# A routed feed-forward and biased attention kernel: trees routed by products, denser slots for tree groups and attention tiles

## What is computed

```python
# attention: x is (4, 512, 128), 16 heads of 8
xn = layernorm(x)                                  # both parts start from normalised tokens
scores = q @ k.T * scale + relative_position_bias  # per batch and head, 512 x 512
out = softmax(scores) @ v @ w_proj.T + b_proj
# feed-forward: four binary trees q, k, v, f of depth 8, over 2048 tokens
for _ in range(8):
    logit = (x * nw[node]).sum(-1) + nb[node]
    node = 2 * node + 1 + (logit > 0)
leaf = node - 255                                  # 256 leaves
y_tree = relu(x @ w1[leaf] + b1[leaf]) @ w2[leaf] + b2[leaf]     # gelu in tree f
# attention over the FFN's tokens: softmax(q k.T / sqrt(128)) v, added to xn, gives y; then y + tree_f(y)
# the output is the sum of both parts
```

## Time and profile before

| | |
|---|---|
| median of 3 runs | 713.75 us (712.23 to 715.29) |
| the profiled execution | 716.28 us, its span 714.6 us |
| PE busy | 576.0 us (81%) |
| DVE busy | 441.7 us (62%) |
| ACT busy | 336.8 us (47%) |
| POOL busy | 255.1 us (36%) |
| mean granted PE clock | 0.942 of 2.4 GHz |

### The profile page before, as it was taken

How to read it: one execution, slowest core, us unless ns; L and a number is a source line. 1 busy time by engine, 2 the same in 40 slices (tenths; PEclk the granted TensorE clock), 3 DMA queues, 4 the chain that set the end, 5 groups by cost and what they waited for, 6 DMA issues and landing times.

```text
span 714.6 us, 11516 instructions
## 1 busy us (share of the span) xinstructions
PE 576.0 (81%) x3540; PEld 413.1 (58%) x3540; DVE 441.7 (62%) x1024; ACT 336.8 (47%) x738; POOL 255.1 (36%) x242
## 2 busy tenths in 40 slices
PE   2276644799999999999999898998976898989930
PEld 0164532577777777776767655656643466666620
DVE  2959987657576666666667556555768565555300
ACT  5520001455555545464646554545223378878720
POOL 4401766750006578267003820000000776000285
PEclk9998758899999999999999999999999799999985
DMA  7979541275657778788551210000000357445123
GB/s 222 253 170 218 215 134 44 54 198 154 163 148 207 195 196 164 184 186 188 155 160 42 34 16 15 1 1 1 0 1 0 112 111 168 133 134 143 41 34 76
DMA packets 108828, 83.42 MB, mean 117 GB/s; under 512 B 8688, under 2 KB 105840, under 8 KB 108768
## 3 DMA queue, kind: packets, MB, share of 16 engines
q1 hardware_dynamic: 93472, 70.07, 37.0%
q0 software_dynamic: 15104, 12.63, 9.6%
q10 hardware_dynamic: 192, 0.00, 0.0%
HBM read 58.30 MB, written 24.36 MB: 116 GB/s over the span
## 4 chain that ended last, share of the span: by engine, by line
PE 59%; DVE 8%; issue 5%; ACT 5%; POOL 4%; DMA 0%; POOLq 0%; DVEq 0%; ACTq 0%
PE ps L983 8%; PE ps L960 7%; PE ps L971 7%; PE ps L973 7%; PE ps L1037 7%; PE ps L1047 6%; POOL xr L386 3%; PE ps L943 3%; DVE ps L618 2%; PE ps L1090 2%; PE ps L1042 2%; ACT hr L797 2%; PE ps L1031 2%; PE ps L998 1%; PE ps L1097 1%
## 5 line engine op out<-in xcount | busy, mean ns | idle before, releaser
L618 DVE CUSTOM_DVE_ANT_0 ps<-ps,strip 128x512 f32<-128x512 f32 x256 | 176.9, 701 | 132.7 <-PE ps L960 128.4
L786 ACT ACTIVATE pt<-ps 128x512 f32<-128x512 f32 x256 | 150.7, 600 | 91.1 <-PE ps L973 89.4
L381 POOL DMA_INDIRECT xs<-xr,slot x64 | 63.4, 990 | 244.6 <-issue 154.8
L971 PE MATMUL ps<-qs,km 128*128 128x512 f32 x256 | 127.1, 497 | 8.4 <-ACT pt L786 7.5
L960 PE MATMUL ps<-km,qs 128*128 128x512 f32 x256 | 111.8, 443 | 15.9 <-DVE mx L618 7.4
L386 POOL DMA_INDIRECT yt<-ys,slot x48 | 74.6, 1555 | 80.5 <-DMA ys<-yl 66.5
L797 ACT ACTIVATE hr<-ps,wt 128x128 f32<-128x128 f32 x192 | 54.7, 368 | 68.0 <-PE ps L1037 68.0
L973 PE MATMUL ps<-u_lo,rev_r 128*128 128x220 f32 (+1 forms) x256 | 74.5, 291 | 0.0
L973 PE MATMUL ps<-u_hi,rev_r 128*128 128x220 f32 (+1 forms) x256 | 73.2, 286 | 0.0
L983 PE MATMUL ps<-pt,v_aug 128*32 128x512 f32 x512 | 69.0, 612 | 0.7 <-ACT pt L786 0.7
L971 PEld LDWEIGHTS ps<-qs,km 128*128 128x128 f32 x256 | 49.0, 191 | 31.2 <-ACT pt L786 19.6
(11 more groups left out here) (207 smaller groups left out, 864.2 us busy)
## 6 DMA issues: line engine op xcount, KB each, us to landing
wt<-in_wl SPq DMA_DIRECT2D x192, 128.5 KB, 2.4
xl<-xs SPq DMA_DIRECT2D x48, 258.0 KB
ys<-yl SPq DMA_DIRECT2D x48, 256.0 KB
xs<-mx SPq DMA_DIRECT2D x2, 3096.0 KB, 23.7
strip<-bias_bf SPq DMA_DIRECT2D x1, 3584.0 KB, 36.2
u_hi<-bias_hi SPq DMA_DIRECT2D x1, 2496.0 KB, 16.1
u_lo<-bias_lo SPq DMA_DIRECT2D x1, 2496.0 KB, 28.5
xs<-xr,slot POOLq DMA_INDIRECT x64
```

Of the source, the lines that this page charges most:

```text
L381: pool.indirect_dma_start(out=xs[t % 2][:, :], out_offset=bass.IndirectOffsetOnAxis(ap=slot[:, t, k:k + 1], axis=0), in_=xr[:, k, :], in_o ...
L618: V.tensor_tensor_reduce(out=bank(u % banks), in0=bank(u % banks), in1=strip[:, HG * g + j, b0:b0 + NS], scale=1.0, scalar=LOWEST, op0=ALU ...
L786: A.activation(pt[:, kt % 2, j, :], bank(2 + u % 2), ACT.Exp).then_inc(S["ex"], 1)
L971: T.matmul(bank(2 + u % 2), km[:, par, j, kt * P:(kt + 1) * P], qs[:, par, :], start=True, stop=False)
```

## The change

It has four parts.

1. **Routing by products.** The logits come out transposed (nodes on partitions, tokens on the free axis). DVE compares two tiles of 128x512 per chunk of 512 tokens (`bits_of`). PE multiplies the bits with a constant path table (`follow`); ACT turns the sums into a one-hot of leaves with a Relu (`leafT`); PE multiplies that with a block table (`settled`), which gives block and leaf. The three trees run as one pipeline of 12 chunks. POOL builds the tables (`tree_edges`, `tree_rows`) and copies the leaf column into the rows ahead of a scatter; before, DVE did, behind a wait for the last scatter.
2. **Tree groups every three slots**, h one slot behind x instead of two, and y four behind instead of five; the groups start 16 slots ahead of slot 0, during the first step's `scores_q`, which go back to two banks.
3. **FFN attention** takes a tile every two slots instead of 2.5, with "o" three slots behind "s"; each batch of values has its own semaphore (`g_v0` to `g_v3`). The eight transposes go one a slot.
4. As a consequence tree f is routed from slot 138 instead of 209 and its groups start at slot 190 instead of 252; the last slot with FFN work is 227 of 320, before 301.

```diff
-LOGIT_BANKS = (2, 3, 4, 5, 6, 7, 0, 1)
+LOGIT_BANKS = ((2, 3), (4, 5))
+PATH_BANKS = (6, 7)
-STAGE_AT = {"x": 0, "h": 2, "m": 3, "y": 5}
-EVERY = 4
-QK_FROM, ATT_FROM, ROUTE_FROM, F_FROM = 150, 167, 209, 252
-ATT_PE, ATT_DVE, ATT_ACT = {"s": 0, "p": 2, "o": 4}, {"s": 0, "o": 4}, {"s": 1, "p": 2}
+STAGE_AT = {"x": 0, "h": 1, "m": 2, "y": 4}
+EVERY = 3
+TREES_FROM, QK_FROM, ATT_FROM, ROUTE_FROM, F_FROM = -16, 95, 103, 138, 190
+ATT_PE, ATT_DVE, ATT_ACT = {"s": 0, "p": 2, "o": 3}, {"s": 0, "o": 3}, {"s": 1, "p": 2}
...
-        for first, start, count in ((0, 0, NTREE * GROUPS), (NTREE * GROUPS, F_FROM, GROUPS)):
+        for first, start, count in ((0, TREES_FROM, NTREE * GROUPS), (NTREE * GROUPS, F_FROM, GROUPS)):
...
-    t, rest = divmod(slot_ - QK_FROM, 2)
-    return [t] if rest == 0 and 0 <= t < 2 * NB else []
+    t = slot_ - QK_FROM
+    return [t] if 0 <= t < 2 * NB else []
...
-    return [(k, i) for i in range(NT) for k, d in reversed(delays.items()) if ATT_FROM + 5 * i // 2 + d == slot_]
+    return [(k, i) for i in range(NT) for k, d in reversed(delays.items()) if ATT_FROM + 2 * i + d == slot_]
...
+            def tree_edges():
+
+                settle(G.iota(n1, [[P, 2]], base=1, channel_multiplier=1, allow_small_or_imprecise_dtypes=True))
+                settle(G.iota(row, [[1, LEAVES]], base=0, channel_multiplier=0, allow_small_or_imprecise_dtypes=True))
+                settle(G.memset(wd, float(LEAVES)))
+                for lv in range(1, 8):
+                    settle(G.tensor_scalar(one, n1, float(1 << lv), -float(1 << (8 - lv)), ALU.is_ge, ALU.mult))
+                    settle(G.tensor_tensor(wd, wd, one, ALU.add))
...
+            def tree_rows():
+
+                b8 = row.rearrange("p (j r) -> p j r", r=LB)[:, :, 0]
+                for h in range(2):
+                    settle(G.tensor_scalar(paths[:, h], row, mid[:, h:h + 1], 2.0, ALU.is_ge, ALU.mult))
+                    for edge in (first, end):
+                        settle(G.tensor_scalar(tmp, row, edge[:, h:h + 1], None, ALU.is_ge))
+                        settle(G.tensor_tensor(paths[:, h], paths[:, h], tmp, ALU.subtract))
...
+                pool.sem_inc(S["tc"], 1)
...
+                settle(G.tensor_copy(xr[:, :, P], part_of[:, t, :]))
...
+            tree_edges()
             far_rows()
+            tree_rows()
...
-                V.tensor_copy(slot[:, t, :], st[:, 5, :])
-                if t:
-                    dve.wait_ge(S["d_sc"], 16 * NT * t)
-                V.tensor_copy(xr[:, :, P], whole[:, 0:NT]).then_inc(S["sl"], 1)
+                V.tensor_copy(slot[:, t, :], st[:, 5, :]).then_inc(S["sl"], 1)
...
+            def bits_of(i):
+
+                t, c = divmod(i, CHUNKS)
+                for h in range(2):
+                    dve.wait_ge(S["lg"], 2 * i + h + 1)
+                    V.tensor_scalar(bitsT[:, h, c * NS:(c + 1) * NS], bank(LOGIT_BANKS[i % 2][h]), nbT[:, t, h:h + 1], None,
+                                    ALU.is_gt).then_inc(S["bit"], 1)
...
+            for i in range(NTREE * CHUNKS + 3):
+                if i < NTREE * CHUNKS:
+                    bits_of(i)
+                t, c = divmod(i, CHUNKS)
+                if c == 1 and t > 0:
+                    places(t - 1, t1)
+                if c == 2 and t > 0:
+                    for _ in ranked(t - 1, t1, (0, 1)):
+                        pass
...
+            def logits(i):
+
+                t, c = divmod(i, CHUNKS)
+                if i >= 2:
+                    pe.wait_ge(S["bit"], 2 * i - 2)
+                for h in range(2):
+                    T.matmul(bank(LOGIT_BANKS[i % 2][h]), nws[t][:, h * P:(h + 1) * P], xn2T[:, c * NS:(c + 1) * NS],
+                             start=True, stop=True).then_inc(S["lg"], 1)
...
+            def settled(i):
+
+                t, c = divmod(i, CHUNKS)
+                pe.wait_ge(S["oh"], 2 * i + 2)
+                if c == 0 and t > 0:
+                    pe.wait_ge(S["rt"], t)
...
+            pe.wait_ge(S["tc"], 1)
...
+            for i in range(NTREE * CHUNKS + 3):
+                if i < NTREE * CHUNKS:
+                    logits(i)
+                t, c = divmod(i, CHUNKS)
+                if c == 2 and t > 0:
+                    ranks(t - 1, t1, (0, 1))
+                if 1 <= i <= NTREE * CHUNKS:
+                    follow(i - 1)
+                if 2 <= i <= NTREE * CHUNKS + 1:
+                    settled(i - 2)
...
-            for u in range(U):
-                scores_q(0, u, 0, 4)
+            for at in range(SLOTS):
+                if at >= LAG:
+                    scores_q(0, at - LAG, 0)
+                for k, i in stages(slot_of(-1, at)):
+                    stage(k, i, i % 2)
```

167 lines of the change are left out of this document (110 added, 57 removed).

## The result

The change makes the kernel slower. The changed kernel took 731.5 us in the median of 4 runs (729.3 to 741.0) against 713.7 for the kernel before in the same session, a ratio of 1.024 with an interval of 1.020 to 1.027. A second session gave 734.5 us and 1.027 (1.024 to 1.031). The prediction was 703 with a range of 684 to 719. The profile shown is that of the second session (the run a0_after_again, the same kernel, span 731.9 us), because the profiled execution of the first session was a slow one (741.0 us, left out of the ratio).

A forecast was written before the change was run, and what follows sets the result against it. PE was taken as the limit in the three trees' stretch, chains and POOL's last gathers elsewhere. Terms -12 + 18 + 44.5 - 42 - 19 = -10.5 gave 705.8 from 716.28, or 703 from the 713.75 median; range 684 to 719.

The forecast's parts named there:

- routing: Ahead of the main loop: routing by products brings the first `scores_q` at 107.5 instead of 119.5, -12 us, bounds -5 and -17.
- the slots ahead of step 0: Slots -16 to -1: three group loops at 6.8 us, 20.4 in all; +18 us for this stage, step 0 at 141.
- slots 0 to 93: Stretch of the three trees' groups: 203 us long against 158.5, +44.5 us, of which 22 are waiting.
- behind slot 94: Rest of the main loop, before 390.7 us: no tree groups -31, attention tiles -11, tree f's groups -1, transposes +1; -42.
- the end: After the main loop: `add_out` no longer waits for POOL's gathers and starts 0.1 us after its product, -19.0 us.
- I take 6.4 us a group: Tree groups: y of one group, weight loads, then h two groups later form a loop of 6.2 to 6.6 us.
- Rival 2: Tree groups: weight-loading loop gets longer, POOL's gathers beside it; a loss from 6.7 us a group, worst 732; chance 0.13.
- a slot without FFN work costs 1.085 us, 21.7 a step: Main loop: slots 0 to 93 less 23.25 groups at 2.43 us of PE leave 102 us for 94 slots.
- I expect 1.9: FFN attention tiles: from 2.6 to 1.9 us each with "o" ahead of the next "p", -11 us, between -15 and +3.
- Tree f's groups: Behind slot 94: 12 groups took 41 us; ACT is the limit, so a group's cost stays, -2 to +6, taken as -1.
- Routing of tree f: Behind slot 94: 29 us before, the same DVE chain after, so no change.
- The 2.4 us for a lower clock at the start of routing: Start of routing: PE comes from idle, so the first 5 us run at the lower clock level, costing 2.4 us.

The follow-up runs named there:

- h1: Changed kernel with three of four of GpSimd's gathers for the trees left out, scatters kept (FFN output not the reference's): 724.1 us, ratio 1.012.
- g2: e1 with only the three trees' groups every third slot, y of a group issued ahead of h of the next: 696.7 us, ratio 0.975.
- f4: Changed kernel with FFN attention as before, a tile every two and a half slots, tree f's routing and groups eight slots later: 735.5 us, ratio 1.029.
- f1: Changed kernel with all schedule numbers of the kernel before; routing by products, leaf column on GpSimd and finer gather semaphores stay: 702.8 us, ratio 0.984.
- e1: Changed kernel with tree groups every four slots, the stage delays of before, and later starts for attention and tree f: 674.0 us, ratio 0.944.
- g1: e1 with its first group in slot 0 instead of -16 and all that follows 16 slots later: 689.8 us, ratio 0.966.
- e2: Changed kernel with y of a group issued ahead of h of the next group in the same slot: 697.8 us, ratio 0.975.
- f2: e2 with weights loaded only for the first two groups of the trees and of tree f (FFN output not the reference's): 675.5 us, ratio 0.947.
- f3: Changed kernel without token-row loads behind the first two groups of the trees and of tree f (FFN output not the reference's): 729.8 us, ratio 1.024.
- h2: e2 with three of four of GpSimd's gathers for the trees left out (FFN output not the reference's): 688.3 us, ratio 0.963.

## Why the prediction was wrong

The sum is made against the profiled executions: 705.8 us less 1.7 around the span is 704.1, and the span is 731.9, 27.8 above. By the prediction's own terms: routing +2.6 better, the slots ahead of step 0 2.3 worse, slots 0 to 93 14.0 worse, behind slot 94 17.2 worse, the end 3.0 better.

**The failed step is the loop, "I take 6.4 us a group".** The mechanism was right: each of its members stands in the fences above. Its size was that of an undisturbed loop. By the rows, from y to the first issue 1.24, the issues 1.93, then 2.2 or 2.8 to h, and 1.0 from h to y: 6.4 without GpSimd's transfers beside it and 7.0 with them. The prediction had 6.2 with the median landing and 6.6 with 2.9 for the latest of four, took the middle, and did not ask what GpSimd's queue does in the same stretch, though 17 of the 24 loops that waited had its transfers beside the gap. The measured mean is 6.95, and y(35) comes at 358.3, where 143.5 + 198 + 2 = 343.5 was foretold.

The 31 distances from y(4) to y(35) sum to 215.5 us, for 200.4. One is 10.9, at the batch's border, where 8.4 was allowed; one is 8.9; the last is only 3.7, since no h stands in front of y(35). The 28 others are 6.86 in the mean and make 12.8 of the 15.1 us. Slots 0 to 93 took 217.0 us for 203. Of these 14 us, h1 gives 6.2 back (349.2 less 138.4 is 210.8), with its scatters and a quarter of the gathers left. The remaining 7.8 no run takes apart.

Rival 2 had the right place (from y(n) to h(n+2), "POOL's gathers beside it"), and its chance of 0.13 was too low. That its worst price, 732, is nearly the measured time is luck: it gets there with 7.2 us a group (its own terms with a landing of 3.3 sum to 7.0), while 6.95 gives 15 of the 28 us, and the others lie behind slot 94. Nor did the DMA share rise by a tenth: it is 0.68 in slots 0 to 93 before and after.

**The second failed step is "a slot without FFN work costs 1.085 us, 21.7 a step".** It was worked out by taking PE's share of a group, 2.43 us, off a full step. A free step takes 22.4 (the row 661.60:684.00). Over the 11.3 steps behind slot 94 that is 8 us. In the same row PE is busy 20.4 of the 22.4; a group in such a step can fill part of the other 2.0, and at four slots it cost 2.3 us, less than its own 2.43 (argued from these rows, not tried by itself). Shown by g2 is what follows for the spacing in this kernel: a group at three slots costs 0.6 us more than at four, and the steps that come free behind the trees take 22.5 all the same, so nothing comes back.

**The third is the attention tiles: with "o" one slot ahead of the next "p", "I expect 1.9".** They were to fall from 2.6 to 1.9 us. Steps 5 and 6 took 41.6 and 43.5, less two free steps and 1 for transposes 39.3, 2.5 a tile: 9 us of the 11 did not come. The tiles start 4.5 us apart in the mean (3.4 to 5.1, once 7.4), for 4.0. f4 shows the same from the other side: at 2.5 slots a tile the time does not change. Which wait holds the tiles is open.

**The rest behind slot 94.** Tree f's groups took 112.8 - 67.2 = 45.6 us for 12, 3.8 each and 5.6 more than the 40 foretold. Routing of tree f took 72.0 - 44.8 = 27 instead of 29. With 8 for the free steps and 9 for the attention these make 21, for a measured 17.2 (from 357.6 to the loop's last copy at 723.46, 365.9 for 348.7). The sum is too high by some 4 us; it counts the last step as a whole free one, and that took 17.0 us (706.46 to 723.46).

**What was right, and what was luck.** Routing by products: -12 predicted, -12.3 by f1. In the trace the first `scores_q` comes 14.6 us earlier. The 2.4 us for a lower clock at the start of routing were not paid: from 42.2 to 50.0 the granted clock is 1.00. Step 0 came at 140.6 for 141, but by two errors that cancel: routing 2.6 better, the stage behind it 2.3 worse. In that stage the clock was 0.90 and not 0.72, and y to y still took 6.4, 7.25 and 7.35 us for the 6.8 taken: what was allowed for the clock went to the loads, in all three loops beside GpSimd's transfers. (The prediction's check with the lower level throughout has a slip: h and y in 3.4 instead of 1.7 us is 3.9 us over its 20.4 for three loops, not 2.) The tail: 19.0 predicted; the last window is 8.5 us where 11.4 were left, where the timeline has one output transfer (729.21, 0.37 us), and before had four in a row (704.33, 4.60 us); this is the likely cause, and not tested. The tables of GpSimd came in time: its last instruction on them ends before L455 starts at 37.0, and the first logits, at 42.3, wait for DVE.

**Where e1's 40 us come from.** Routing 12.3 (f1). From f1 to g1, denser attention and tree f earlier, 13.1, of which the tail gives 12.6 (6.5 us of the 19.1 are left in g1), so the attention gives about nothing, as f4 says. From g1 to e1, groups ahead of step 0, 15.8: 6.5 are the rest of the tail and 9 the loop. That these make up e1's 41 us is no check, since each is the difference of neighbouring kernels; and f1, g1 and e1 are of three sessions, in which the kernel before took 715.2, 713.5 and 715.1. All but the attention's part are in the prediction; the spacing of three slots with its stage order took them back and 19 us more. Of the 60 us between e1 and the changed kernel, the order within the slot is 37 (e2) and the spacing 24 (e2 less e1). e1 has the lowest median of the study; f2's, without most of the weight loads, is not told apart from it.

The rule of the Trainium skill that bears on the failed step is in DMA: Bandwidth & Descriptors, section "Queues, rings and completion order": each transfer engine takes turns between the queues that have work for it. Read against this change it says that SP's weight loads and GpSimd's gathers hold each other up where they meet on an engine. h1 agrees: without three quarters of the gathers the kernel is 10.4 us faster, 6.2 of them in slots 0 to 93. The prediction had that neighbourhood in view only in rival 2, and priced it there by a share of busy time.

## What to carry to other kernels

A loop that ends in a transfer is to be priced with the latest landing of its group, read in the stretch where the other queues are as busy as they will be, and then compared with the work that covers it; from there each 0.1 us is paid in every round. The queue that issues the transfers has a turn of its own, with the reads between its issues, and when the loop gets shorter it is the next to end last: SP's 5.5 to 6.2 us here. Work that fills gaps is worth spreading: before filler is packed more densely, measure what a step costs without it (22.4 us here) and what one piece costs inside (2.3), and ask what the freed steps will hold. When several edits come together, run each alone: here 12 us from routing and 28 from the hidden tail and the start ahead of step 0 were covered by a spacing and a stage order that lost 60.

## What the runs showed of the hardware

A wait that is removed can appear in another engine. With y first, PE's wait for weights fell from 34.9 to 11.4 us, and DVE's wait for the store `ys` rose from 3.1 to 44.8.

Four weight loads of 128.5 KB each, issued back to back in 1.93 us, let h start 2.2 us after the last issue ends where GpSimd starts no indirect transfer in that gap, and 2.8 us after it where it does (means of 7 and 17 loops).

Ahead of routing, GpSimd's tensor_tensor of 128x2048 again holds an instruction of DVE for its whole length, now a cast of 128x128 with a single input, from the timelines of POOL and of DVE:

```profile
37.02 4.51 POOL L455 TENSOR_TENSOR acc<-acc,att 128x2048 f32<-128x2048 f32 x1 [0.27 <-POOL b_pT L408]
...
37.15 4.52 DVE L561 CAST rev_r<-cst 128x128 fp32r<-128x128 f32 x1
```

That the cast is held and not slow is shown by other runs with the same code: in f2, f3, f4 and h2 GpSimd's instruction starts only at 37.7 to 38.4, the cast runs ahead of it in 0.27 to 0.28 us, and the first logits come at 40.4 to 40.9. In the nine others of the fourteen the first logits come at 42.1 to 42.5, in f1 at 43.2. In the earlier trace rows it was an instruction of eight columns, held 3.52 us, where the same line takes 0.17 us elsewhere in that trace. It has one input, as the cast has, so the rule on two SBUF inputs that the prediction names is not its case. The prediction had priced the hold at nothing because some instruction was held either way; the first logits came at 42.3, where it had 44.1, but without the hold they come about 2 us sooner.
